# Cross-attention and mixture of experts: where the first dispatch runs, how the expert weights are split, who issues the stores, and how late the gathers run

## What is computed

```
x = x + tanh(g_xattn) * attention(layernorm(x), ctx)      # 16 heads of 16, rope, softmax, output projection
h = layernorm(x)
p = softmax(h @ w_router)                                 # 16 experts, the best 2 for each token
buf[e, slot] = h[token]                                   # dispatch: 16 slots per expert and sequence, overflow dropped
o = (silu(buf @ w_gate) * (buf @ w_fc)) @ w_proj          # per expert, hidden size 128
x = x + tanh(g_ffn) * sum_k p_k * o[e_k, slot_k]          # collect
```

## Time and profile before

| | us |
|---|---|
| median of 3 runs | 1701.09 |
| lowest and highest | 1697.56, 1702.18 |
| the profiled execution | 1707.24 |
| its span | 1705.5 |

### The profile page before, as it was taken

One profiled execution on the slowest core, in us unless ns is written; L12 is line 12 of the kernel. 1 busy time (PEld: TensorE's weight loads), 2 busy tenths in 40 slices (PEclk: granted clock), 3 DMA queues, 4 the chain that ended last, 5 costly groups with the idle time before them and its releaser, 6 DMA issues. The chain is left out here.

```text
span 1705.5 us, 50836 instructions
## 1 busy us (share of the span) xinstructions
PE 1492.2 (87%) x16928; PEld 1219.5 (72%) x16928; DVE 1412.9 (83%) x3262; ACT 1172.7 (69%) x2289; POOL 981.3 (58%) x1478
## 2 busy tenths in 40 slices
PE   3999999999999999999999999985698888888880
PEld 3677777777777777777777777763598878788870
DVE  3789999999999999998999999985777777777753
ACT  3778787787877878778787877874465555555540
POOL 3566666666666666666666666652025555555565
PEclk9999999999999999999999999995699999999995
DMA  3134412212122121221212212110258888788876
GB/s 100 51 120 136 142 66 68 87 61 92 61 73 81 61 92 61 75 78 61 92 61 78 76 62 92 62 51 25 73 182 266 261 255 264 249 263 257 263 231 204
DMA packets 137544, 210.47 MB, mean 123 GB/s; under 512 B 16625, under 2 KB 69873, under 8 KB 137457
## 3 DMA queue, kind: packets, MB, share of 16 engines
q1 hardware_dynamic: 106736, 142.29, 26.3%
q0 software_dynamic: 12288, 33.57, 6.6%
q10 hardware_dynamic: 18432, 33.56, 5.5%
HBM read 125.47 MB, written 83.89 MB: 123 GB/s over the span
## 5 line engine op out<-in xcount | busy, mean ns | idle before, releaser
L597 DVE TRANSPOSE_TENSOR_REDUCE part_max<-ST 128x16 f32<-128x512 f32 x512 | 320.6, 683 | 17.8 <-PE ST L843 17.7
L425 ACT ACTIVATE probs_t<-ST 128x512 f32<-128x512 f32 x512 | 264.3, 603 | 19.9 <-PE ST L858 15.6
L1210 POOL DMA_INDIRECT first<-eo_d,code x128 | 133.3, 1042 | 201.3 <-DVE xr L1322 108.2
L870 PE MATMUL PO<-probs_t,v_aug 128*32 128x128 f32 x4096 | 180.5, 283 | 2.4 <-issue 2.1
L1333 PE MATMUL GU<-we_hi,s_hi 128*128 128x256 f32 x512 | 156.5, 306 | 0.0
L1210 POOL DMA_INDIRECT second<-eo_d,code x128 | 122.4, 956 | 41.7 <-issue 37.7
L1334 PE MATMUL GU<-we_hi,s_lo 128*128 128x256 f32 x512 | 145.9, 285 | 0.0
L1335 PE MATMUL GU<-we_lo,s_hi 128*128 128x256 f32 x512 | 145.7, 285 | 0.0
L336 POOL TENSOR_TENSOR k_rot<-k_cos,k_sin 128x256 f32<-128x256 f32 x64 | 46.9, 734 | 161.0 <-DVE k_sin L635 161.0
L1333 PE MATMUL EO<-we_hi,h_hi 128*128 128x256 f32 x256 | 79.1, 309 | 68.8 <-ACT h_hi L1225 42.4
L431 ACT ACTIVATE out_t<-PO 128x512 f32<-128x512 f32 x128 | 76.7, 599 | 89.7 <-PE PO L870 89.7
(11 more groups left out here) (155 smaller groups left out, 5730.6 us busy)
## 6 DMA issues: line engine op xcount, KB each, us to landing
eo_d<-eo ACTq DMA_DIRECT2D x128, 256.0 KB
x_in_sb<-x SPq DMA_DIRECT2D x64, 256.0 KB, 2.8
c_in_sb<-ctx_t SPq DMA_DIRECT2D x64, 256.0 KB, 2.9
xr_sb<-x SPq DMA_DIRECT2D x64, 256.0 KB, 4.1
x_d<-x SPq DMA_DIRECT2D x64, 256.0 KB, 4.1
xn_d<-xn SPq DMA_DIRECT2D x64, 256.0 KB, 3.8
raw<-xn_d SPq DMA_DIRECT2D x64, 256.0 KB
xr<-x_d SPq DMA_DIRECT2D x64, 256.0 KB
```

What stands on the lines that cost most here:

```text
L425: act.activation(probs_t[:, b, i].rearrange("p j q -> p (j q)"), ST[i][:], ACT.Exp) \
L597: dve.tensor_reduce(part_max[:, i, 0], ST[i][:].rearrange("p (c l) -> p c l", l=32), AX_X, ALU.max, apply_transpose=True).then_inc(M["part ...
L870: last = pe.matmul(PO[32 * j:32 * j + 32, i * SEQ:(i + 1) * SEQ], v_aug[:, n.par, b, head], probs_t[:, b, i, j], start=True, stop=True)
L1210: pool.indirect_dma_start(out=dst[:, n.turn(3)], out_offset=None, in_=D["eo_d"][n.group].rearrange("r e c -> (r e) c"), in_offset=bass.Ind ...
```

## The change

- The expert block's steps become functions (`sp_step` and so on), which the attention block calls too. Units -14 to -2 (the first eight dispatches among them) run in the attention's drain, after the steps of pairs 63 to 67. The expert block begins with unit -1.
- SP's first load there waits for `rest_done`, for all of `pv_done` and for the landing of the first `xn2` stores. The tiles of the dispatch lie over tiles of the attention that are done with (`over`), and `DS` uses two PSUM banks of the scores.
- The pieces of the weights are spread otherwise. ACT: 0 behind the first exponentials of pair 63, 1 to 3 ahead of the last ones, 4 to 9 in step 64, 10 and 11 in step 65. DVE: 0 and 1 to 3 in step 63, 4 to 7 in step 64, then one piece in each of the steps 66 to 69.
- SP issues the store of `eo`, not ACT.
- FETCH and COLLECT have lags 12 and 14 where they had 13 and 15, so there is one unit fewer.

```diff
+    early = {PAIRS - 1: (-14, -13, -12), PAIRS: (-11, -10, -9, -8), PAIRS + 1: (-7, -6), PAIRS + 2: (-5, -4),
+             PAIRS + 3: (-3, -2)}
...
         for c in range(PAIRS - 4, PAIRS + 9):
             step(Pair(0, c))
+            for u in early.get(c, ()):
+                dispatch(u)
...
+        def dispatch(u):
+            if u == -14:
+                sp.wait_ge(M["rest_done"], 16)
+                sp.wait_ge(M["pv_done"], SEQS * 4)
+                for q in xn2_out:
+                    sp.wait_ge(q, 16 * 8)
+            X["sp"](sp, unit_at(u), on_at(u))
...
+            if s.beyond == 0:
+                weight_heads(4, 6)
             if (s - 2).real:
                 normed2(s - 2)
             if quad(s, 4):
                 exp_logits(quad(s, 4))
-            if s.beyond == -1:
-                weight_heads(0, 3)
             if (s - 1).real:
                 attention_head(s - 1)
+            if s.beyond == 0:
+                weight_heads(6, 8)
             if s.real:
                 for i in range(4):
                     exp_unit(s, 0, i)
-            if s.beyond == 0:
-                weight_heads(8, 10)
+            if s.beyond == -1:
+                weight_heads(0, 1)
...
             if s.beyond == -1:
-                weight_heads(3, 8)
+                weight_heads(1, 4)
             if s.beyond == 0:
+                weight_heads(8, 10)
+            if s.beyond == 1:
                 weight_heads(10, CH)
...
+            if s.beyond == 0:
+                weight_rests(4, 5)
             if s.real:
                 shift_of(s, 0)
-            if s.beyond == -1:
-                weight_rests(0, 3)
...
             if s.beyond == 0:
-                weight_rests(7, 8)
+                weight_rests(5, 7)
             route_early(s)
+            if s.beyond == -1:
+                weight_rests(0, 1)
...
             if s.beyond == -1:
-                weight_rests(3, 7)
+                weight_rests(1, 4)
             if s.beyond == 0:
-                weight_rests(8, CH)
+                weight_rests(7, 8)
+            if s.beyond is not None and s.beyond > 1 and s.beyond < 6:
+                weight_rests(s.beyond + 6, s.beyond + 7)
...
+        def dispatch(u):
+            if u == -11:
+                dve.wait_ge(M["place_done"], 4)
+            X["dve"](dve, unit_at(u), on_at(u))
...
-    LOAD, PICK, HEAD, REST, DISPATCH, GATE, HIDDEN, OUTPUT, FETCH, COLLECT = -14, -11, -11, -10, -9, 0, 2, 3, 13, 15
+LOAD, PICK, HEAD, REST, DISPATCH, GATE, HIDDEN, OUTPUT, FETCH, COLLECT = -14, -11, -11, -10, -9, 0, 2, 3, 12, 14
...
+    def sp_step(sp, unit, on):
+        n = unit(OUTPUT)
+        if on(OUTPUT):
+            sp.wait_ge(M["eo_copied"], n.n + 1)
+            sp.dma_start(D["eo_d"][n.group][:, n.j * 2:n.j * 2 + 2], eo[n.turn(3)][:]) \
+                .then_inc(eo_out[n.turn(3)], 16)
...
-            n = unit(OUTPUT)
-            if on(OUTPUT):
-                act.wait_ge(M["eo_copied"], n.n + 1)
-                act.dma_start(D["eo_d"][n.group][:, n.j * 2:n.j * 2 + 2], eo[:, n.turn(3)]) \
-                    .then_inc(eo_out[n.turn(3)], 16)
```

More of the change, by code:

```diff
@@ L1200, in _ @@
-    @block.gpsimd
-    def _(pool):
-        def step(unit, on):
-            n = unit(FETCH)
-            if on(FETCH):
-                pool.wait_ge(M["collect_done"], 1)
-                for r, q in enumerate(eo_out):
-                    pool.wait_ge(q, len(range(r, (n.group + 1) * GROUP, 3)) * 16)
-                wait_for(pool, M["out_done"], n.n - 2)
-                for k, dst in ((0, first), (1, second)):
-                    pool.indirect_dma_start(
-                        out=dst[:, n.turn(3)], out_offset=None,
-                        in_=D["eo_d"][n.group].rearrange("r e c -> (r e) c"),
-                        in_offset=bass.IndirectOffsetOnAxis(ap=collect_row[:, k, n.n:n.n + 1], axis=0)) \
-                        .then_inc(rows_in[n.turn(3)], 16)
-        run_flat(pool, step)
@@ new lines, in pool_step @@
+    def pool_step(pool, unit, on):
+        n = unit(FETCH)
+        if on(FETCH):
+            pool.wait_ge(M["collect_done"], 1)
+            for r, q in enumerate(eo_out):
+                pool.wait_ge(q, len(range(r, (n.group + 1) * GROUP, 3)) * 16)
+            wait_for(pool, M["out_done"], n.n - 2)
+            for k, dst in ((0, first), (1, second)):
+                pool.indirect_dma_start(
+                    out=dst[:, n.turn(3)], out_offset=None,
+                    in_=D["eo_d"][n.group].rearrange("r e c -> (r e) c"),
+                    in_offset=bass.IndirectOffsetOnAxis(ap=collect_row[:, k, n.n:n.n + 1], axis=0)) \
+                    .then_inc(rows_in[n.turn(3)], 16)
@@ new lines, in dve_step @@
+        n = unit(PICK)
+        if on(PICK) and n.n == 0:
+            dve.wait_ge(iota_in, 16)
+        if on(PICK) and n.n % 2 == 0:
+            wait_for(dve, M["ds_done"], n.n - 2)
+            dve.tensor_tensor(two(pick, n, 4).rearrange("p b (e s) -> p b e s", s=CAP),
+                              place[:, bass.ds(n.n, 2)].rearrange("p b (e s) -> p b e s", s=1)
+                              .broadcast_to([P, 2, EXPERTS, CAP]),
+                              iota[:].rearrange("p (b e s) -> p b e s", b=1, s=CAP)
+                              .broadcast_to([P, 2, EXPERTS, CAP]), ALU.is_equal) \
+                .then_inc(M["pick_done"], 1)
@@ L1382, in _ @@
-        run(pe, step)
+        n = unit(OUTPUT)
+        if on(OUTPUT):
+            for done in ("h_hi_done", "h_lo_done"):
+                pe.wait_ge(M[done], n.n + 1)
+            wait_for(pe, M["eo_copied"], n.n - 1)
+            for e in range(2):
+                at = n.j * (2 * DIM) + e * DIM
+                last = split_matmul(EO[n.slot(2)][:, e * DIM:(e + 1) * DIM],
+                                    [h[:, n.slot(2), e] for h in (h_hi, h_lo)],
+                                    [w[:, at:at + DIM] for w in w_down])
+            last.then_inc(M["eo_done"], 1)
@@ new lines, in pe_step @@
+        n = unit(DISPATCH)
+        if on(DISPATCH):
+            for done in ("pick_done", "x_hi_done", "x_lo_done"):
+                pe.wait_ge(M[done], n.pair + 1)
+            wait_for(pe, M["s_lo_done"], n.n - 1)
+            slot = n.slot(4)
+            for k in range(KC):
+                out = DS[n.slot(2)][:, k * SLOTS:(k + 1) * SLOTS]
+                pe.matmul(out, x_hi[:, slot, k * P:(k + 1) * P], pick[:, slot], start=True, stop=False)
+                last = pe.matmul(out, x_lo[:, slot, k * P:(k + 1) * P], pick[:, slot],
+                                 start=False, stop=True)
+            last.then_inc(M["ds_done"], 1)
```

398 lines of the change are left out of this document (189 added, 209 removed).

## The result

| | before | after |
|---|---|---|
| median us (9 runs each, timed together) | 1701.09 | 1695.00 |
| lowest and highest | 1697.33, 1703.14 | 1687.99, 2876.56 |
| ratio, 95% interval | | 0.9965 [0.9949, 0.9980] |
| the profiled execution, its span | 1707.24, 1705.5 | 1697.39, 1695.6 |

The change makes the kernel 6.1 us faster; by the interval it can be 3 to 9 us. One run of the nine took 2876.56 us; the median and the interval don't hang on it. I forecast 1690, a gain of 11.4 us: inside the range, but a good half of the gain is all that came.

What follows compares the result with a forecast made beforehand. Transfers were taken to pace the expert stage, a chain through all engines the drain, POOL the tail. Drain 9.0 us plus tail 2.4, all else nothing, gave 11.4 us off 1701.09: 1690 us, range 1674 to 1704.

Steps and rivals of the forecast that it cites:

- The drain: Between attention and experts: the drain ends 9.0 us later but saves the dispatch after it; first `GU` 9.0 us sooner (5 to 15).
- POOL's four instructions: POOL's scale in the drain, from `ve` to the end of `off`: 2.7 us where it took 4.35.
- my sum of 21.4: Last logits to last `place`: 7.9 us as before plus 13.5 for three pairs of dispatches and four weight pieces.
- SP's waits: SP's first loads in the drain, behind `pv_done`: cost nothing; if late, one landing of about 3.1 us, once.
- FETCH and COLLECT: At the tail, one sequence fewer is left when PE stops: 2.4 us won of POOL's 2.6 us row.
- nothing, if the stage pays: Lower end of the tail's gain: 0 us if the expert stage pays for the transfers of the sequence gathered sooner.
- Stores from SP: In the expert stage, ACT is freed of 0.46 us in each of 128 units: taken as nothing, between 0 and 18 us.
- The rule that I weighed: DMA queues: one row is consumed in ring order, so SP's stores stand behind two loads and an `out` store: 1712.
- the third rival: Stores come late at the starts of 15 groups, POOL waits 1.5 us each, 22 us lost: 1712; chance 0.15.
- A stage that the transfers pace: Expert stage: transfers set the unit of 3.53 us, about 908 KB at 257 GB/s, DMA share 0.81; unit stays 3.5 us.
- shorter cycle: First rival, expert stage: ACT's freed 0.46 us shortens recovery after each stall, 18 us more: 1672; chance 0.20.
- lengthened by what it saves: Second rival, drain: grows by 16 us or more, only 0 to 2 us plus the tail remain: 1699; chance 0.15.

Runs made afterwards that it cites:

- experiment 3: The changed kernel with the stores of `eo` issued by ACT again and lags 13 and 15 again, leaving only drain and weights: 1689.93 us, ratio 0.9936.
- three pairs of kernels: ACT's against SP's stores: new drain, lags 13 and 15 (1689.93, 1698.95 us); kernel before, alone with SP's stores (1709.25 us); changed kernel's lags (1690.28, 1695.00 us).
- experiment 11: The changed kernel with the stores of `eo` on ACT, and the loads of `xr` and, from unit 2, `raw` moved to ACT too: 1703.13 us, ratio 1.0013.
- experiment 7: The changed kernel with ACT's stores of `eo`, and each finished sequence stored a second time into a spare tensor: 1695.23 us, ratio 0.9971.
- experiment 10: The changed kernel with all 256 indirect gathers replaced by plain reads of the same bytes, other rows, from the same queue: 1608.28 us, ratio 0.9454.
- experiment 1: The changed kernel with the stores of `eo` issued by ACT again, lags still 12 and 14: 1690.28 us, ratio 0.9929.
- experiment 12: The changed kernel with only the second gather of each sequence made a plain read: 1616.15 us, ratio 0.9900; the kernel before beside it took 1632.27 us.

## Why the prediction was right or wrong

**The drain: right.** Forecast for the last exponentials 1158.1, measured 1160.28; for the last output's transposes 1166.7, 1168.12; for POOL's four instructions 2.7 us, 3.13; for `xn` 1184.4, 1185.92, behind the two `s_hi` as argued; for the logits 1189.3, 1190.76; for the end of the last `place` 1210.7, 1210.41; for the first `GU` 1212.2, 1212.02. The last exponentials waited 1.15 us for PE's `ST`, which my sum of ACT's and DVE's pieces left out; the 2.2 us are the largest error, and shrink to 1.5 by the logits. The part from the logits to the end of `place` took 19.65 us, 1.75 less than my sum of 21.4. Two of its terms were off. I had DVE do 14.8 us of dispatches and weights in that part and hide 1.3 us of them in its waits. It did 11.4 us more than before there, and its idle time didn't shrink (1190.76 to 1210.41 of the changed kernel, 1193.83 to 1201.70 of before):

```profile
1190.76:1210.41 19.65, 7.39 (x36) 6.07 (x36) 17.52 (x45) 6.56 (x12) 5.79 (x10) 0.50 0.14 41
1193.83:1201.70 7.87, 1.34 (x12) 0.74 (x12) 6.14 (x29) 0.26 (x1) 2.96 (x10) 0.50 0.00 0
```

So the drain is right in its chain and nearly right in its parts, and the end at 1212.0 for 1212.2 is in part luck: a start 1.5 us late and a part 1.75 us short cancel. Gain forecast 9.0 us, in the traces 9.2; alone, in the medians of experiment 3, 11.7, of which the weights may be about 2.

**SP's waits: right.** The loads in the drain cost nothing: `xn` was held by PE's products, and the first `GU` came 1.6 us behind the end of the last `place`, 1.5 forecast.

**FETCH and COLLECT: right in the trace, wrong in the sum.** The tail is 2.8 us shorter, 2.4 forecast. But I took that for the kernel's gain, and named "nothing, if the stage pays" as the lower end only. With the stores on ACT that end is what happened (1689.93 and 1690.28). With the stores on SP the lags bring 4.0 us by the medians, with intervals that just overlap; if they do, why is open.

**Stores from SP: the step that failed.** I put them at nothing, with ends of 0 and a gain of 18 us. They cost 9.0, 8.45 and 4.7 us in three pairs of kernels. I had seen the 1 us at which the `out` store could hold them up, but priced it only against the slack of the group's first gather, where it seems to have cost nothing: POOL's wait for `eo_d<-eo` is 14.5 us in 15 times with SP's stores at these lags, and 24.4 us in 15 in experiment 3, with ACT's stores and a shorter stage. The loss lies inside the units: 4.6 to 4.7 us of stage in the traces of all three pairs, of which 2.7 to 3.4 are PE's busy time at a clock that falls six to eight times and not one to three. My sum had no term for the clock in the stage. Taking one side of an unknown cost as zero was the error; the row that I had (an engine with idle time gives up an issue of 0.33 us) bounds only the gain.

The rule that I weighed, in the Trainium skill (DMA: Bandwidth & Descriptors, section "Queues, rings and completion order"), says that each DMA engine consumes one row in ring order; a store that shares its row with loads then stands behind those that were issued before it. It spoke against the change, and the sign was as it says. The time isn't that of the third rival, though, since POOL's waits for the stores are not longer by it, and experiment 11 failed to isolate the shared row. So the runs neither confirm nor refute it as the cause. What I set against the rule, that no store had been seen to hold up a gather, was a misreading. The trace of before has such waits from 1300 to 1640:

```profile
POOL first L1210 <- DMA eo_d<-eo: 9.7, 9, 1.3
```

**"A stage that the transfers pace": wrong.** More bytes left the unit at 3.5 us (experiment 7), and the same bytes without indirection went through in 2.83 (experiment 10). The forecast that the unit stays at 3.5 us was right for a wrong reason. That reason mattered: "the bytes are the same" is the ground on which I took nothing for the stores' move. If bytes had set the unit, who issues a transfer could have been worth little; I hadn't asked what a store that comes later does to a unit that is held by waits.

**The rivals.** No shorter cycle came, a gain of 18 us. The drain wasn't lengthened by what it saves. The third rival had the right part of the change and the right sign, but the wrong place (starts of groups) and a price of 22 us where 5 to 9 were measured.

**A version that beats both**: experiments 1 and 3, 1690.28 and 1689.93 us. It is the change without the move of the stores; the lags don't matter then. My 1690 us are what these two kernels take; the changed kernel doesn't.

## What to carry to other kernels

When a part of a change is forecast at zero, time the kernel without it: here one part brought 11.7 us and another gave 5 to 9 of them back, and a square of four kernels shows what each costs with and without the other. When a stage's time changes, compare the busy time of the bound engine for the same instructions, and its granted clock, before looking for waits: more than half of this loss stood there. A high DMA share beside idle engines doesn't say that bytes are the bound; add bytes, and if the unit doesn't lengthen, look for another cause. Before a transfer is moved to another engine's queue, list the waits that move with it and what stands behind them there (69 us of waits on ACT that cost SP nothing).

## What the runs showed of the hardware

- With 256 indirect gathers of 128 KB the units of the stage took 3.54 us, and with as many plain reads of other rows from the same queue, with the same packets, 2.83, with PE busy 99.6% of the time. That is 87 us of 1695. I hadn't expected a transfer's kind to reach PE. It was so while the kernel before took 1701 us (see the last point).
- The DMA engines carried 321 GB/s at a share of 0.96 with plain reads. With indirect gathers they carried 256 at 0.81, and 297 at 0.92 with one store more in each unit (experiment 7).
- In the stage the granted clock fell from 1.00 to 0.50 (2.4 to 1.2 GHz) for a few us behind pauses of PE: eight times from 1260 to 1640 in the changed kernel, three times in experiment 1, and not once from 1260 to 1577 in experiment 10, where PE hardly pauses. In each of the three pairs five more such falls go with 2.7 to 3.4 us more busy time of PE for the same matmuls.
- In the last of the four sets of experiments the kernel before took 1632 us, its runs as close together as elsewhere, and in the other three 1701. The attention was the same. The 69 us lie, by the estimate in experiment 12, in the stage with the indirect gathers. A comparison across sets of runs would have been wrong by 4%.

A page that I hadn't used in the prediction bears on the first of these. The Trainium skill (SBUF — State Buffer, section "Who interferes with whom") says that DMA never contends with a compute engine. Where the reads were plain the trace agrees: PE is busy 259 us of 260 at 321 GB/s. Where they were indirect PE lost 0.7 us a unit (experiment 12's kernel before, by estimate, didn't); the trace doesn't show that this happens at a port, so it doesn't refute the sentence, but who reads "no contention" as "no cost to the compute engines" would have missed the largest term of this kernel.
